# Attention bias of an eight-core transformer layer moved from a VectorE add to two rank-one TensorE matmuls

## What is computed

```python
xn = layernorm(x)
q = (xn @ Wq).reshape(b, s, 32, 128);  k, v = split(xn @ Wkv)
scores = einsum('bqhd,bkd->bhqk', q, k) * 128**-0.5
scores = where(causal, scores + slope[h] * (k_pos - q_pos), -inf)
attn = softmax(scores);  out = einsum('bhqk,bkd->bqhd', attn, v) @ Wo
# gated branch: top 16 of 64 experts from a 16-wide router, z = xn @ A^T gated, then @ B^T * 2
x + out + branch
```

## Time and profile before

| | us |
|---|---|
| median of the 2 runs | 5606.5 |
| lowest, highest run | 5525.4, 5687.7 |
| the profiled execution, its time | 5530.2 |
| its span on core 1 (all cores: 5493.8 to 5528.6) | 5528.6 |
| PE matmul busy | 3529.8 (64%) |
| DVE busy | 1496.0 (27%) |
| ACT busy | 1085.7 (20%) |

### The profile page before, as it was taken

How to read it: one execution, slowest core, us unless ns; L and a number is a source line. 1 busy time by engine, 2 the same in 40 slices (tenths; PEclk the granted TensorE clock), 3 DMA queues, 4 the chain that set the end, 5 groups by cost and what they waited for, 6 DMA issues and landing times.

```text
span 5528.6 us, 49638 instructions; the slowest of 8 cores (5493.8 to 5528.6 us)
## 1 busy us (share of the span) xinstructions
PE 3529.8 (64%) x17216; PEld 1724.9 (31%) x17216; DVE 1496.0 (27%) x3505; ACT 1085.7 (20%) x1984; POOL 165.7 (3%) x171
## 2 busy tenths in 40 slices
PE   1576566666634499963766666656655545558999
PEld 1332222222222244432322222333333222223444
DVE  4211222222234300023122223333333444442000
ACT  4001111111133300012011222222222333331000
POOL 0000000000000000000000000000000000000000
PEclk9887777777755599976887777767767666668999
DMA  5343232232151158733422212112115000002764
GB/s 115 62 61 55 47 55 42 37 54 47 32 101 41 37 114 150 144 100 99 61 47 47 47 38 41 32 32 39 32 27 82 17 24 17 17 17 60 153 138 99
DMA packets 293247, 340.03 MB, mean 62 GB/s; under 512 B 28688, under 2 KB 249872, under 8 KB 282640
## 3 DMA queue, kind: packets, MB, share of 16 engines
q0 software_dynamic: 244480, 163.75, 22.5%
q1 hardware_dynamic: 30096, 139.54, 7.7%
q10 hardware_dynamic: 18432, 33.56, 1.6%
HBM read 467.01 MB, written 33.55 MB: 91 GB/s over the span
## 4 chain that ended last, share of the span: by engine, by line
PE 54%; DVE 16%; issue 13%; ACT 9%; DMA 8%; DVEq 1%; ACTq 0%; SPq 0%; POOLq 0%
PE ps_a L426 19%; PE ps_a L663 16%; DVE scratch L589 9%; PE ps_c L549 7%; ACT astream L597 6%; PE ps_t L513 3%; DMA wstream<-wq 3%; DMA scratch<-x 3%; PE ps_s L582 2%; DVE scratch L523 2%; PE ps_a L668 2%; DVE cols L602 1%; DVE cols L196 1%; ACT scratch L526 1%; ACT astream L222 1%
## 5 line engine op out<-in xcount | busy, mean ns | idle before, releaser
L549 PE MATMUL ps_c<-scratch,vT 128*128 128x256 bf16 x1959 | 544.7, 381 | 1115.6 <-DVE scratch L523 561.1
L426 PE MATMUL ps_a<-xnT,wstream 128*128 128x512 bf16 x4096 | 1080.5, 430 | 78.0 <-DMA wstream<-wq 78.0
L597 ACT ACTIVATE astream<-scratch,cols 128x384 bf16<-128x384 f32 (+15 forms) x512 | 534.0, 1043 | 2208.1 <-DVE scratch L589 2207.4
L663 PE MATMUL ps_a<-xnT,QC 128*128 128x512 bf16 x4096 | 906.3, 379 | 1.7 <-ACT QC L557 1.7
L589 DVE TENSOR_TENSOR scratch<-ps_s,scratch 128x512 f32<-128x512 f32 (+3 forms) x1088 | 609.2, 593 | 266.1 <-PE ps_s L582 248.7
L582 PE MATMUL ps_s<-kT,QC 128*128 128x512 bf16 (+3 forms) x1088 | 399.4, 427 | 440.4 <-DVE scratch L589 438.0
L426 PEld LDWEIGHTS ps_a<-xnT,wstream 128*128 128x128 bf16 x4096 | 447.3, 110 | 681.6 <-issue 318.2
L549 PEld LDWEIGHTS ps_c<-scratch,vT 128*128 128x128 bf16 x1959 | 167.1, 114 | 1293.4 <-issue 1280.5
L663 PEld LDWEIGHTS ps_a<-xnT,QC 128*128 128x128 bf16 x4096 | 401.0, 98 | 486.1 <-issue 4.2
L513 PE MATMUL ps_t<-identsb,astream 128*128 128x128 bf16 x3593 | 493.1, 291 | 0.0
L513 PEld LDWEIGHTS ps_t<-identsb,astream 128*128 128x128 bf16 x3593 | 400.7, 136 | 99.1 <-issue 28.4
(11 more groups left out here) (62 smaller groups left out, 1146.9 us busy)
## 6 DMA issues: line engine op xcount, KB each, us to landing
scratch<-ab SPq DMA_DIRECT2D x65, 1088.0 KB, 5.1
wstream<-wq POOLq DMA_DIRECT2D x64, 1024.0 KB, 13.8
xnT<-wo POOLq DMA_DIRECT2D x64, 1024.0 KB, 28.6
scratch<-x SPq DMA_DIRECT2D x16, 2048.0 KB, 8.3
scratch<-x SPq DMA_DIRECT2D x128, 256.0 KB, 4.4
out<-scratch ACTq DMA_DIRECT2D x128, 256.0 KB, 4.6
astream<-awt POOLq DMA_DIRECT2D x16, 1024.0 KB, 10.7
wstream<-bwt POOLq DMA_DIRECT2D x16, 512.0 KB, 38.5
```

Source lines behind the costliest of these rows:

```text
L426: E.matmul(ps_a[b][:], wq_half_view[hh][:, kk % 16, mm * 128:(mm + 1) * 128], xnT[:, kk, t2 * 512:(t2 + 1) * 512], start=(kk == 0), stop=( ...
L549: E.matmul(ps_c[b][:, 0:256], vT[:, jj * 128:(jj + 1) * 128], u[:, c0:c0 + 256], start=st, stop=fin), inc="pe")
L597: ac_exp = p.op("scalar", lambda E, ss=us, pp=par, LL=L: E.activation(v_un[ss][:, 0:LL], v_sp[pp][:, 0:LL], AF.Exp, bias=c_negB, accum_out ...
L663: p.op("tensor", lambda E, b=bank, kk=k, pp=par, tt=t: E.matmul(ps_a[b][:], QC[:, kk, tt * 128:(tt + 1) * 128], wo_view[pp][:, kk, :], sta ...
```

## The change

The position bias is separable: slope*(k - q) = slope*k - slope*q. The key part becomes a row of 2176 numbers for each head, split into a bf16 value and its remainder; each of the two rows is added to the scores inside PSUM by a matmul whose stationary operand is one row of ones (contraction over one partition). The query part becomes the per-partition bias operand of the exponential. Only the diagonal 128 x 128 piece still gets an add on DVE, of a constant causal mask, from PSUM to PSUM. The exponential reads PSUM directly, once for each chunk of up to 512 columns, each chunk with its own row sum, and DVE adds the sums. The bank `ps_s` is released by the exponential. The bias load is 17 KB of f32 in DRAM to one partition as bf16, on the POOL queue; PE waits for it at the head's start, and it may start after the last bias matmul of the head before. Two constants (`tri`, `ioc`) are loaded once at the start.

```diff
+    ld_tri = p.op("gpsimd", lambda E: E.dma_start(out=tri[:], in_=dtri), inc="dgp", incby=16)
+    ld_ioc = p.op("gpsimd", lambda E: E.dma_start(out=ioc[:], in_=dioc), inc="dgp", incby=16)
...
-        p.need("sync", ("abbuf",))
-        ab_ds = p.op("sync", lambda E: E.dma_start(out=v_ab, in_=dab[0]),
+        p.need("gpsimd", ("abbuf",))
+        ab_ds = p.op("gpsimd", lambda E: E.dma_start(
+            out=v_brow, in_=dbh[0:1].rearrange("h a b -> h (a b)")),
             inc="dsab", incby=16)
         for h in range(H):
             qdrain_through(h // 2)
-            p.wait("vector", "dsab", ab_ds)
+            p.wait("tensor", "dsab", ab_ds)
...
+            dv_bq = p.op("vector", lambda E, sl=SLOPES[h], b=hb: E.tensor_scalar(
+                c_bq[b], ioc[:], -sl, -40.0, ALU.mult, ALU.add), inc="dv")
...
-                            start=True, stop=True), inc="pe")
-                        p.wait("vector", "pe", pe_sc)
-                        dv_tt = p.op("vector", ... E.tensor_tensor(
-                                         v_sp[pp][:, cc * 512:cc * 512 + w],
-                                         ps_s[b][:, 0:w], v_ab[:, ao:ao + w], ALU.add),
-                        p.release(("ps_s", bank), "dv", dv_tt)
-                    ac_exp = p.op("scalar", ... E.activation(
-                        v_un[ss][:, 0:LL], v_sp[pp][:, 0:LL], AF.Exp,
-                        bias=c_negB, accum_out=c_Z[ss]), inc="ac")
+                            start=True, stop=False), inc="pe")
+                        p.op("tensor", ... E.matmul(
+                            ps_s[b][:, 0:w], onesr[:], v_brow[:, bo:bo + w],
+                            start=False, stop=False))
+                        pe_sc = p.op("tensor", ... E.matmul(      # bo is 2176 further
+                            ps_s[b][:, 0:w], onesr[:], v_brow[:, bo:bo + w],
+                            start=False, stop=True), inc="pe")
+                        if ci == nch - 1:
+                            gate_val = p.op("vector", ... E.tensor_tensor(
+                                ps_s[b][:, dc:dc + 128], ps_s[b][:, dc:dc + 128],
+                                tri[:], ALU.add), inc="dv")
+                        exp_last_ac = p.op("scalar", ... E.activation(
+                            v_un[ss][:, cc * 512:cc * 512 + w], ps_s[b][:, 0:w], AF.Exp,
+                            bias=c_bq[bb], accum_out=c_zc(ss, cc)), inc="ac")
+                        p.release(("ps_s", bank), "ac", exp_last_ac)
+                    dv_z = p.op("vector", ... E.reduce_sum(
+                        c_Z[ss], cols[:, 24 + ss * 4:24 + ss * 4 + n], axis=AX.X), inc="dv")
...
-            p.release(("abbuf",), "dv", last_tt_dv)
+            p.release(("abbuf",), "pe", last_bias_pe)
             if nxt is not None:
-                p.need("sync", ("abbuf",))
-                ab_ds = p.op("sync", ... E.dma_start(out=v_ab, in_=dab[hh]),
+                p.need("gpsimd", ("abbuf",))
+                ab_ds = p.op("gpsimd", ... E.dma_start(out=v_brow, in_=dbh[hh:hh + 1]...),
```

More of the change, by code:

```diff
@@ L93, in build_program @@
     dkeyst = nc.dram_tensor("keyst", [RD, NE], F32, kind="ExternalInput").ap()
-    dab = nc.dram_tensor("ab", [H, 128, S + 128], F32, kind="ExternalInput").ap()
+    dbh = nc.dram_tensor("bh", [H, 2, S + 128], F32, kind="ExternalInput").ap()
+    dtri = nc.dram_tensor("tri", [128, 128], F32, kind="ExternalInput").ap()
+    dioc = nc.dram_tensor("ioc", [128, 1], F32, kind="ExternalInput").ap()
     dident = nc.dram_tensor("ident", [128, 128], F32, kind="ExternalInput").ap()
@@ L122, in build_program @@
     m8b = sb("m8b", [128, 8], F32)
-    cols = sb("cols", [128, 32], F32)
+    cols = sb("cols", [128, 48], F32)
+    tri = sb("tri_sb", [128, 128], F32)
+    ioc = sb("ioc_sb", [128, 1], F32)
+    onesr = sb("onesr", [1, 128], BF16)
     stats = sb("stats", [128, 8], F32)
@@ L146, in build_program @@
     c_negB = cols[:, 23:24]
+    c_zc = lambda s, ci: cols[:, 24 + s * 4 + ci:25 + s * 4 + ci]
+    c_bq = [cols[:, 40:41], cols[:, 41:42]]
     c_nm = [cols[:, 10 + i:11 + i] for i in range(4)]
@@ L178, in build_program @@
                     inc="dgp", incby=16)
+    ld_tri = p.op("gpsimd", lambda E: E.dma_start(out=tri[:], in_=dtri), inc="dgp", incby=16)
+    ld_ioc = p.op("gpsimd", lambda E: E.dma_start(out=ioc[:], in_=dioc), inc="dgp", incby=16)
+    p.wait("vector", "dv", dv_eps)
+    dv_ones = p.op("vector", lambda E: E.memset(onesr[:], 1.0), inc="dv")
     for c in range(2):
@@ L471, in build_program @@
             qdrain_through(h // 2)
-            p.wait("vector", "dsab", ab_ds)
+            p.wait("tensor", "dsab", ab_ds)
+            p.wait("tensor", "dv", dv_ones)
+            hb = h % 2
+            p.wait("vector", "dv", dv_eps)
+            p.need("vector", ("bq", hb))
+            dv_bq = p.op("vector", lambda E, sl=SLOPES[h], b=hb: E.tensor_scalar(
+                c_bq[b], ioc[:], -sl, -40.0, ALU.mult, ALU.add), inc="dv")
+            p.wait("vector", "dgp", ld_ioc)
+            p.wait("scalar", "dv", dv_bq)
             W = WIN[h]
@@ L580, in build_program @@
                         p.need("tensor", ("ps_s", bank))
-                        pe_sc = p.op("tensor", lambda E, b=bank, hh=h, qq=qt, k0=kb_lo,
-                                     cc=ci, w=colw: E.matmul(
+                        broff = kb_lo - q0 + S + ci * 512
+                        p.op("tensor", lambda E, b=bank, hh=h, qq=qt, k0=kb_lo,
+                             cc=ci, w=colw: E.matmul(
                             ps_s[b][:, 0:w], QC[:, hh, qq * 128:(qq + 1) * 128],
                             kT[:, k0 + cc * 512: k0 + cc * 512 + w],
-                            start=True, stop=True), inc="pe")
@@ new lines, in build_program @@
+                        p.op("tensor", lambda E, b=bank, bo=broff, w=colw: E.matmul(
+                            ps_s[b][:, 0:w], onesr[:], v_brow[:, bo:bo + w],
+                            start=False, stop=False))
+                        pe_sc = p.op("tensor", lambda E, b=bank, bo=broff + 2176, w=colw:
+                                     E.matmul(
+                            ps_s[b][:, 0:w], onesr[:], v_brow[:, bo:bo + w],
+                            start=False, stop=True), inc="pe")
@@ new lines, in build_program @@
+                        last_bias_pe = pe_sc
+                        gate_sem, gate_val = "pe", pe_sc
+                        if ci == nch - 1:
+                            dcol = (L - 128) - ci * 512
+                            p.wait("vector", "pe", pe_sc)
+                            gate_val = p.op("vector", lambda E, b=bank, dc=dcol:
+                                            E.tensor_tensor(
+                                ps_s[b][:, dc:dc + 128], ps_s[b][:, dc:dc + 128],
+                                tri[:], ALU.add), inc="dv")
+                            gate_sem = "dv"
@@ new lines, in build_program @@
+                        p.wait("scalar", gate_sem, gate_val)
+                        p.need("scalar", ("un", us))
+                        exp_last_ac = p.op("scalar", lambda E, b=bank, ss=us, cc=ci,
+                                           w=colw, bb=hb: E.activation(
+                            v_un[ss][:, cc * 512:cc * 512 + w], ps_s[b][:, 0:w], AF.Exp,
+                            bias=c_bq[bb], accum_out=c_zc(ss, cc)), inc="ac")
+                        p.release(("ps_s", bank), "ac", exp_last_ac)
@@ L602, in build_program @@
+                    p.release(("bq", hb), "ac", exp_last_ac)
+                    p.wait("vector", "ac", exp_last_ac)
+                    dv_z = p.op("vector", lambda E, ss=us, n=nch: E.reduce_sum(
+                        c_Z[ss], cols[:, 24 + ss * 4:24 + ss * 4 + n], axis=AX.X),
+                        inc="dv")
+                    p.wait("vector", "dv", dv_z)
                     dv_rz = p.op("vector", lambda E, ss=us: E.reciprocal(c_rz[ss], c_Z[ss]),
@@ L614, in build_program @@
             nxt = h + 1 if h < H - 1 else (0 if c == 0 else None)
-            p.release(("abbuf",), "dv", last_tt_dv)
+            p.release(("abbuf",), "pe", last_bias_pe)
             if nxt is not None:
-                p.need("sync", ("abbuf",))
-                ab_ds = p.op("sync", lambda E, hh=nxt: E.dma_start(out=v_ab, in_=dab[hh]),
-                             inc="dsab", incby=16)
+                p.need("gpsimd", ("abbuf",))
+                ab_ds = p.op("gpsimd", lambda E, hh=nxt: E.dma_start(
+                    out=v_brow,
+                    in_=dbh[hh:hh + 1].rearrange("h a b -> h (a b)")),
+                    inc="dsab", incby=16)
         while qpend:
@@ L713, in _host_constants @@
 def _host_constants():
-    if "ab" not in _CACHED:
+    if "bh" not in _CACHED:
+        import ml_dtypes
         krel = np.arange(-S, 128, dtype=np.float32)
-        i = np.arange(128, dtype=np.float32)
[L717 to L721, removed]
+        bh = np.empty((H, 2, S + 128), dtype=np.float32)
```

(9 more changed lines are left out.)

22 lines of the change are left out of this document (5 added, 17 removed).

## The result

The changed kernel is slower: 1.0239 of the kernel before, 95% interval 1.0188 to 1.0291 (slower beyond doubt, by 2% or more not quite). Its profiled execution has a span of 5646.1 us against 5528.6. (The medians, 5713 against 5591, hold executions in which one die ran slower; ratios are of undisturbed ones.)

The account below looks back on a forecast made before the run. The prediction took the serial path of each attention pair, 7.25 us from first score to copy, as the bound, with no engine busy throughout. 5530.2 - 204 + 66 = 5392, say 5390 us; own range 5310 to 5470, wide range 5270 to 5600.

Parts of the forecast that it names:

- the worked pair: Attention pair of 896 and 1024 keys, first score to copy: 5.9 us warm, 7.6 cold, against 7.5 before.
- The price of a rank-one matmul: PE, bias matmuls: each priced like a 128-row one, so a chunk costs 0.65 us warm or 1.28 cold.
- Which clock: PE in attention: which pairs run warm or cold; with the other matmuls' gain, -204 us together.
- the 120 as warm: The 120 pairs that follow a projection group were taken to run at the warm clock: -113 us.
- shares of a quarter to 0.6 for the rest: The other 136 pairs: short ones cold, longer ones warm by a quarter, a half and 0.6: -66 us.
- -25 for the other matmuls: Transposes, value products and projection groups gain from the clock, 120 groups at about 0.2 us: -25 us.
- the first rival: PE clock follows used array rows, not time, so it does not hold: +50 us, 5580 us, chance 0.20.
- the clock rival: The rival that the PE clock does not hold, summed as -56-1+41+66 = +50 us; chance 0.20.
- 22 forecast: First half's output projection: wo loads queued on POOL behind the bias loads add 22 us of new wait.
- 30+11 forecast: wq loads: 30 us of later issue before heads 4, 8, 12, 16, plus 11 given back at existing waits.
- The bias row: Bias load at each head's start: hidden under 7 us of transposes and values, so 0 us.
- both rivals on it (10.5 and 18.6): Bias load landing in 10.5 us: +143, 5535 us, chance 0.10; in 18.6 us: +590, 5980 us, chance 0.07.

Follow-up runs that it names:

- e4: Changed kernel without its bias matmuls and with a constant query bias, so the position bias is left out: ratio 0.9356 to the kernel before, span 5190.8 us.
- e1: Changed kernel with both bias matmuls' operands over 128 partitions (row 0 as before, other rows zero): span 5285.9 us.
- e5: Changed kernel with the score matmul last in every second chunk, halving the changes of operand height: ratio 1.0098 to the kernel before.
- e8: Changed kernel with both bias matmuls' operands over 64 partitions: ratio 1.0125 to the kernel before.
- e2: Changed kernel with the bias row stored as bf16 in DRAM and loaded from the SP queue: ratio 1.0037 to the kernel before, span 5558.8 us.
- e9: Changed kernel with one 128-row bias matmul per chunk (value and remainder in rows 0 and 1) and the bf16 bias load on SP: span 5201.4 us.

## Why the prediction was wrong

**The bound and the pair.** Right in kind. The pair is the unit, and taking the adds off DVE shortens it: e4 shows 338 us for the change without its matmuls. I read the series of the two blocks on DVE, but not that the mask add kept it. In the worked pair the second block's last chunk "meets DVE free at 3.5"; in pairs with one chunk per block that is where it waits. With that series still in it, e1, whose matmuls cost what was priced and whose clock rose, took 5286, about 100 below the 5390 that were added up. Whether its pairs gained more than priced or only had more of the clock (0.90 in the late heads) stays open.

**The price of a rank-one matmul.** The upper end was right for two in a row (0.40 us of start to start for 512 columns at 1.2 GHz, 0.43 priced), and the Trainium skill's rule (TensorE: Matmul & The Clock Gate, "Why this matters for your kernels") that a matmul over 32 rows takes as long as one over 128 agrees with this trace for such neighbours, here of one row. The sum left out what stands between neighbours of different height: 0.14 and 0.13 us of exposed weight load per chunk, 130 to 156 us by e5. Cold pairs of 896 and 1024 keys were forecast at 7.6 and took 8.09.

**Which clock.** This is the step that failed: "the 120 as warm", with shares of a quarter to 0.6 for the rest and -25 for the other matmuls, -204 in all. The changed kernel had 0.75, 0.51, 0.74 and 0.59, against the 0.77, 0.52, 0.74 and 0.63 of the earlier trace rows, where above 0.8 had been forecast for the first and third and above 0.7 for the last. I took busy time as what holds the clock; e1 shows with nothing but height changed that it is the rows too, and e8 that they count with the exposed loads left in. It was the first rival ("the clock may follow used rows"), which I gave 0.20 and 5580. The measured 5646 lies beyond it and above the range's 5600, because the exposed weight loads were in no case. With POOL's waits taken off (36.5 and 125.1-78.0 = 47.1), attention lost 117.5-83.6 = 34 us; the clock rival's own sum for it was -56-1+41 = -16, 50 off. As the exposed loads alone are 130 to 156, the rest of that sum was 80 to 106 too high: it came near by two errors that partly cancel, and e4's 338 us, above the 180 to 280 expected, point to the gain of the pairs as the one that was priced too low. The reason I gave against the rival, that the trace has no such matmul, was a reason for neither side, and should have made the two cases about equal.

**POOL's queue.** Right in kind, too low in size (63 forecast for `Wo` and `wq`, 84 measured as waits). `Wo`: 22 forecast, 36.5 measured: the cover was 9.5 us (1966.5 to 2012.5 less the 36.5), not 13, and the loads took 45.5 from their issue, not 34. PE needs the first strip of `Wo` and the `B` load issued behind it (L681), and the wait is put down to `B`. `wq`: 30+11 forecast, 47 measured. The bias row: 0, measured 0, with a landing of 1.9 us; both rivals on it (10.5 and 18.6) fall. e2 gives 87 for all of it against a forecast of 63.

## What to carry to other kernels

A low operand is not a cheap one. If a matmul of few rows alternates with full ones and the chain is near PE's pace, lay it over all 128 partitions with zeros, and put several rank-one terms into one matmul. Look for what an in-order engine does between two independent blocks: moving one 128-column add off DVE's queue gave 270 us once PE had slack, and 84 while it had little. A load that waits for the end of a loop's pass does not belong on a queue that also prefetches.

## What was not expected of the hardware

- The granted clock of heads 20 to 31, second half, is 0.59 with one-row, 0.71 with 64-row and 0.90 with 128-row bias matmuls, PE being 80, 78 and 67% busy. With full-height matmuls alone it is 0.62 without bias matmuls (e4, PE 64% busy), 0.80 with one per chunk (e9) and 0.90 with two: operands that are nearly all zeros raised the clock above that of the kernel without them. A dense run of one third full and two thirds one-row matmuls fell from 2.4 to 1.2 GHz right behind a projection group.
- A change between operand heights exposes the weight load: 0.57 us from start to start instead of 0.43 for 512 columns at 1.2 GHz, and 0.31 instead of 0.22 at 2.4 GHz (3995.93 to 3996.24). With 64 rows the 0.57 is the same (e8).
- A load of 17 KB of f32 to one partition as bf16 (8.5 KB there) from POOL landed in 1.9 us, while the 32 KB load at the kernel's start takes 10.5: a start-up row does not bound a later one.
